# Five output banks, both rank-8 results in one bank, and the rank-8 result's low part made on GpSimd

## The reference

```python
# layer 3 (the last): rank-8 update of a base matrix, per batch
xw = gelu(layernorm(cond) @ w1 + b1) @ w2 + b2
x_a, x_b = split(xw)                          # (16, 512, 8) each
layer = base_layer + x_a[b] @ x_b[b].T        # per batch b
out = x3 + x3 @ layer
```

## Time and profile before

| | |
|---|---|
| median of 3 runs | 1496.57 us (1495.63 to 1499.19) |
| profiled execution | 1498.06 us, of which span 1496.1 us |
| busy in the span | TensorE 1422.0 us (95%), VectorE 1006.8, GpSimd 682.1, ScalarE 659.6 |
| mean granted TensorE clock | 0.977 of full speed |

### The profile page before, as it was taken

How to read it: one execution, slowest core, us unless ns; L and a number is a source line. 1 busy time by engine, 2 the same in 40 slices (tenths; PEclk the granted TensorE clock), 3 DMA queues, 4 the chain that set the end, 5 groups by cost and what they waited for, 6 DMA issues and landing times.

```text
span 1496.1 us, 49921 instructions
## 1 busy us (share of the span) xinstructions
PE 1422.0 (95%) x21159; PEld 1124.8 (75%) x21159; DVE 1006.8 (67%) x2707; ACT 659.6 (44%) x2185; POOL 682.1 (46%) x536
## 2 busy tenths in 40 slices
PE   6789999999999999999999999999997996999998
PEld 4457888888888888888888888888886874677776
DVE  4333757575757576767676666666656689898884
ACT  3444444545454545444444444444444442233332
POOL 2422444444444444434353535343424355777773
PEclk9799999999999999999999999999997997999999
DMA  9660142423232323333333323242315457888893
GB/s 351 225 245 18 33 84 41 76 49 68 52 65 52 66 51 66 58 59 58 59 61 62 64 54 67 53 70 52 58 31 107 113 112 139 284 316 308 315 329 124
DMA packets 441904, 168.15 MB, mean 112 GB/s; under 512 B 406433, under 2 KB 409633, under 8 KB 438354
## 3 DMA queue, kind: packets, MB, share of 16 engines
q1 hardware_dynamic: 441682, 164.97, 43.6%
HBM read 96.78 MB, written 68.16 MB: 110 GB/s over the span
## 4 chain that ended last, share of the span: by engine, by line
PE 90%; DVE 3%; issue 2%; ACT 2%; POOL 1%; DMA 1%; SPq 0%; ACTq 0%; DVEq 0%; POOLq 0%
PE bank L466 47%; PE recb L432 28%; PE bank L627 12%; PE bank L641 1%; PE bank L513 1%; DMA xt<-in_Wx 1%; ACT gates L813 1%; PE recb L610 1%; PE spare L610 1%; PE aux L478 1%; DVE pre L1150 0%; DVE pre L1148 0%; DVE hs L1155 0%; DVE pout L1214 0%; ACT hs L652 0%
## 5 line engine op out<-in xcount | busy, mean ns | idle before, releaser
L432 PEld LDWEIGHTS recb<-hs,scanS 128*128 128x128 f16 x16384 | 444.7, 96 | 172.6 <-DVE hs L1155 169.8
L432 PE MATMUL recb<-hs,scanS 128*128 128x32 f16 x16384 | 495.3, 177 | 25.9 <-DVE hs L1155 25.9
L652 ACT ACTIVATE hs<-pre 128x64 f16<-128x64 f32 x512 | 131.6, 257 | 621.6 <-DVE pre L1150 620.1
L1148 DVE TENSOR_TENSOR pre<-recb,xw 128x64 f32<-128x64 f32 x512 | 114.9, 224 | 266.6 <-PE recb L432 262.8
L1016 DVE RECIPROCAL gates<-gates 128x64 f32<-128x64 f32 (+1 forms) x484 | 258.1, 554 | 0.4
L1155 DVE TENSOR_TENSOR hs<-konst,hs 128x64 f16<-128x64 f32 x512 | 115.0, 225 | 137.0 <-ACT konst L653 137.0
L875 POOL TENSOR_TENSOR xt<-xt,hbuf 128x512 f32<-128x512 f32 (+1 forms) x65 | 98.8, 1520 | 177.7 <-ACT hbuf L656 177.7
L863 POOL TENSOR_TENSOR x1lo<-xt,x1hi 128x512 fp32r<-128x512 f32 x62 | 80.6, 1301 | 198.8 <-ACT x1hi L662 198.8
L881 POOL TENSOR_TENSOR gates<-gates 128x512 f32<-128x512 f32 x64 | 83.0, 1296 | 165.4 <-DVE gates L1016 165.4
L890 POOL TENSOR_TENSOR xt<-xt,pout 128x512 f32<-128x512 f32 x64 | 76.2, 1191 | 149.6 <-DVE pout L1042 144.5
L1150 DVE TENSOR_TENSOR pre<-recb,pre 128x64 f32<-128x64 f32 x512 | 114.8, 224 | 17.6
(11 more groups left out here) (202 smaller groups left out, 2730.4 us busy)
## 6 DMA issues: line engine op xcount, KB each, us to landing
xt<-in_x SPq DMA_DIRECT2D x64, 256.0 KB, 3.5
g_d<-gst SPq DMA_DIRECT2D x64, 256.0 KB, 3.8
n_d<-nst SPq DMA_DIRECT2D x64, 256.0 KB, 3.1
x_d<-xt SPq DMA_DIRECT2D x64, 256.0 KB, 3.1
out<-gates SPq DMA_DIRECT2D x64, 256.0 KB, 6.5
xt<-x_d SPq DMA_DIRECT2D x28, 512.0 KB, 4.6
stage<-in_w SPq DMA_DIRECT2D x11, 1024.0 KB, 5.8
xt<-g_d SPq DMA_DIRECT2D x14, 512.0 KB, 6.9
```

The costliest lines, as they stand in the source:

```text
L432: last = nc.tensor.matmul(rec[:, m].rearrange("p a b -> p (a b)"), w[:, k, m * P:(m + 1) * P], hs[:, k].rearrange("p a b -> p (a b)"), sta ...
L652: nc.scalar.activation(hs[:, :, 0, :], pre[t % 2][:], ACT.Tanh, scale=unscale).then_inc(s_h, 1)
L1148: nc.vector.tensor_tensor(pre0[:], rec[:, :, 0, :], xw[j % 2][:, t], ALU.add).then_inc(s_pre0, 1)
```

## The change

It makes five banks for the output of the last stage (`obank`: the four and `spare`); quarter t of batch b lies in bank (4b + t) mod 5. Both rank-8 results lie in `recb`, at columns 0 to 127 and 256 to 383. ScalarE makes, beside the high part, a second, whole copy of the rank-8 result in SBUF (`yf`), since GpSimd reads it there, and GpSimd makes the low part from it. The subtraction leaves VectorE's order and stands in GpSimd's behind `x3_low` of the next batch's chunk 1 (for batch 0 behind that of chunk 0).

```diff
--- before.py
+++ after.py
@@ -151,8 +151,13 @@
         scan = [scanS[k // 2][:, k % 2, :] for k in range(4)]
         oout = gates[:, 0:NT]
         ysh, ysl = ([x2hi[:, q, e * P:(e + 1) * P] for q in range(2)] for e in range(2))
+        yf = [xar[:, q * P:(q + 1) * P] for q in range(2)]
         xbs = [x2lo[:, q, :] for q in range(2)]
-        yp = [s[:, 0:P] for s in (recb, spare)]
+        yp = [recb[:, 0:P], turned]
+        obank = bank + [spare]
+
+        def quarter(b, t):
+            return obank[(NT * b + t) % len(obank)]
 
 
         (d_cond, d_w1, d_w2, d_wx, d_wh, d_rows, d_ln, d_h1, d_bias, d_c2, d_f, d_i, d_c) = (
@@ -174,8 +179,8 @@
         d_e = {k: [sem(f"t_d_e{k}{q}") for q in range(2)] for k in "gnx"}
         d_t = {k: [[sem(f"t_d_{k}{q}{h}") for h in range(2)] for q in range(2)] for k in "gnx"}
         d_xbs, d_out = [sem(f"t_d_xbs{q}") for q in range(2)], [sem(f"t_d_out{t}") for t in range(NT)]
-        (s_gc, s_nc, s_xc, s_one2, s_S, s_u, s_H, s_x3, s_x3h, s_x3l, s_pm, s_yp, s_yh, s_yl, s_op, s_o) = (
-            sem("t_" + s) for s in "s_gc s_nc s_xc s_one2 s_S s_u s_H s_x3 s_x3h s_x3l s_pm s_yp s_yh s_yl s_op s_o".split())
+        (s_gc, s_nc, s_xc, s_one2, s_S, s_u, s_H, s_x3, s_x3h, s_x3l, s_pm, s_yp, s_yh, s_yf, s_yl, s_op, s_o) = (
+            sem("t_" + s) for s in "s_gc s_nc s_xc s_one2 s_S s_u s_H s_x3 s_x3h s_x3l s_pm s_yp s_yh s_yf s_yl s_op s_o".split())
 
         made = {"x": s_xp, "f": s_f, "i": s_i, "c": s_c}
 
@@ -598,10 +603,8 @@
                 q = b % 2
                 pe.wait_ge(s_x3, C * b + m + 1)
                 if m == 0:
-                    if b >= 2:
-                        pe.wait_ge(s_yl, b - 1)
-                    elif b:
-                        pe.wait_ge(s_P, 2 * C * NBLK)
+                    if b:
+                        pe.wait_ge(s_yf, b)
                     else:
                         pe.wait_ge(s_x3, C)
                         pe.wait_ge(s_xah, 1)
@@ -617,14 +620,16 @@
                 pe.wait_ge(s_x3h, C * b + m + 1)
                 pe.wait_ge(s_x3l, C * b + m + 1)
                 for t in range(NT):
-                    if m == 0 and b:
-                        pe.wait_ge(s_o, NT * (b - 1) + t + 1)
+                    if m == 0 and NT * b + t == len(bank):
+                        pe.wait_ge(s_P, 2 * C * NBLK)
+                    elif m == 0 and b:
+                        pe.wait_ge(s_o, NT * b + t - len(bank))
                     elif m == 0:
                         kind, chunk = LAST_GROUPS[2 * C + t]
                         pe.wait_ge(emptied(kind), C * (NBLK - 1) + chunk + 1)
                     tok = slice(t * P, (t + 1) * P)
                     for e, (x3, w) in enumerate(((x3hi, bhi), (x3lo, bhi), (x3hi, blo))):
-                        last = nc.tensor.matmul(bank[t][:], x3[q][:, m, tok], w[:, m, :], start=(m == 0 and e == 0), stop=False)
+                        last = nc.tensor.matmul(quarter(b, t)[:], x3[q][:, m, tok], w[:, m, :], start=(m == 0 and e == 0), stop=False)
                 last.then_inc(s_pm, 1)
 
             for b in range(B):
@@ -638,7 +643,7 @@
                 for y, rows in ((ysh, PAIR), (ysl, RANK)):
                     for t in range(NT):
                         part = slice(t * PADB, t * PADB + rows)
-                        last = nc.tensor.matmul(bank[t][:], y[b % 2][part], xbs[b % 2][part], start=False, stop=(y is ysl), tile_position=(t * PADB, 0))
+                        last = nc.tensor.matmul(quarter(b, t)[:], y[b % 2][part], xbs[b % 2][part], start=False, stop=(y is ysl), tile_position=(t * PADB, 0))
                         if y is ysl:
                             last.then_inc(s_op, 1)
 
@@ -805,12 +810,15 @@
                 else:
                     act.wait_ge(s_c, C * NBLK)
                 nc.scalar.copy(ysh[b % 2], yp[b % 2]).then_inc(s_yh, 1)
+                if b >= 2:
+                    act.wait_ge(s_yl, b - 1)
+                nc.scalar.copy(yf[b % 2], yp[b % 2]).then_inc(s_yf, 1)
 
             def put_out(b, t):
                 act.wait_ge(s_op, NT * b + t + 1)
                 if b:
                     act.wait_ge(d_out[t], 16 * b)
-                nc.scalar.copy(oout[:, t, :], bank[t][:]).then_inc(s_o, 1)
+                nc.scalar.copy(oout[:, t, :], quarter(b, t)[:]).then_inc(s_o, 1)
 
             last = NBLK - 1
             for m in range(C):
@@ -959,6 +967,11 @@
                 pool.wait_ge(s_x3h, k + 1)
                 nc.gpsimd.tensor_tensor(x3lo[b % 2][:, m, :], xin[b % 2][:, m, :], x3hi[b % 2][:, m, :].bitcast(F32), ALU.subtract).then_inc(s_x3l, 1)
 
+            def y_low(b):
+                pool.wait_ge(s_yh, b + 1)
+                pool.wait_ge(s_yf, b + 1)
+                nc.gpsimd.tensor_tensor(ysl[b % 2], yf[b % 2], ysh[b % 2].bitcast(F32), ALU.subtract).then_inc(s_yl, 1)
+
             last = NBLK - 1
             for m in range(C // 2):
                 x2_low(last, m)
@@ -985,14 +998,20 @@
             for k in range(C, C + 3):
                 times_n(k)
             x3_low(C)
+            y_low(0)
             times_n(C + 3)
             x3_low(C + 1)
             times_n(C + 4)
             for k in range(C + 5, SLOTS):
                 times_n(k)
                 x3_low(k - 3)
+                if (k - 3) % C == 1:
+                    y_low((k - 3) // C - 1)
             for k in range(SLOTS - 3, SLOTS):
                 x3_low(k)
+                if k % C == 1:
+                    y_low(k // C - 1)
+            y_low(B - 1)
 
         @block.vector
         def _(dve):
@@ -1194,10 +1213,6 @@
                 dve.wait_ge(s_H, k + 1)
                 nc.vector.tensor_tensor(xin[b % 2][:, m, :], xin[b % 2][:, m, :], total, ALU.add).then_inc(s_x3, 1)
 
-            def y_low(b):
-                dve.wait_ge(s_yh, b + 1)
-                nc.vector.tensor_tensor(ysl[b % 2], yp[b % 2], ysh[b % 2].bitcast(F32), ALU.subtract).then_inc(s_yl, 1)
-
             def shares_of(m):
                 gate_sum(last, m)
                 recip(last, m, 0, PIECES)
@@ -1252,7 +1267,6 @@
             hidden(3)
             suffix(C)
             suffix(C + 1)
-            y_low(0)
             hidden(C)
             suffix(C + 2)
             hidden(C + 1)
@@ -1264,9 +1278,6 @@
                 if k + 3 < SLOTS:
                     suffix(k + 3)
                 hidden(k)
-                if k % C == 1:
-                    y_low(k // C - 1)
-            y_low(B - 1)
 
 
 def flat(view):
```

## The result

The changed kernel took 1488.17 us (median of 16 runs, 1485.7 to 1495.02) against 1500.63 for the kernel before in the same comparison: ratio 0.9922, 95% interval 0.9906 to 0.9938, so 0.8% faster. The profiled execution took 1486.39 us with a span of 1484.6 (before: 1498.06 and 1496.1).

What follows compares the result with a forecast made beforehand. Bound: TensorE plus a 0.72 us turnaround at each last-stage batch's end. Gains of 0.6 us at the start and 13 x 0.70 made 9.7 us, so 1486.9 us from the 1496.57 median; range 1483.8 to 1492, chance 0.62.

Steps and rivals of the forecast that it cites:

- Part 1: Handover between last-stage batches: with five output banks quarter 0 needn't wait for a drain, gaining 0.70 us each.
- Part 2: Rank-8 low part moves from VectorE to GpSimd: 0.60 us subtraction there, one more ScalarE copy, no cost to the period.
- the room: Slack between GpSimd's new subtraction and TensorE's rank-8 matmuls in each last-stage batch: 0.22 us.
- The sum: Whole last stage: 0.6 us at its start plus 13 transitions of 0.70 us, 9.7 us gained.
- The start: Batches 0 to 2 of the last stage: batch 2 starts 0.6 us sooner, bounds 0 to 1.5.
- (a): GpSimd's line becomes the last stage's bound: gain of 4.5 to 8 us, chance 0.18; smaller gains share 0.13 with (c).
- (b): Denser transfers in the last stage make n loads land 2 us later, delaying GpSimd: 1506.1 us, chance 0.07.
- (c): Last-stage handover: a later drain holds quarter 1 instead of quarter 0, 1493 to 1497 us; chance 0.13 shared with (a)'s end.
- (d): Denser TensorE work in the last stage lowers the clock; left out, given no size or chance.

Runs made afterwards that it cites:

- one drain more: The changed kernel with one more ScalarE copy of quarter 0 ahead of each batch's first drain, to a place nobody reads: ratio 0.9988 to the kernel before.
- both runs: The changed kernel with one or three more GpSimd subtractions of the same size ahead of each low part: ratios 0.9955 and 1.0008 to the kernel before.
- the banks alone: The changed kernel with VectorE keeping the low part, so only five banks and the shared rank-8 bank: ratio 0.9953 to the kernel before.

## Why the prediction was right

**Time and sign.** Forecast 1486.9 from a median of 1496.57, 0.65% less; the ratio says 0.78% (0.62 to 0.94). 0.65 lies in the interval. The stage alone gained 10.6 us, forecast 9.7. That 1486.9 is so near the measured 1488.17 is in part luck: the kernel before was 4.1 us slower in this comparison than the median that the forecast started from (1500.63 against 1496.57), and the gain was 12.5 in place of 9.7.

**Part 1, 0.70 us a handover.** Measured: from the start of batch 2 to the rank-8 matmuls of batch 15, 191.61 before and 181.94 after, 9.67 / 13 = 0.74. Quarter 0 starts where it was put (0.67 after the start of the rank-8 matmuls). Quarter 1 was put 0.83 behind it with the weights loaded late, its second matmul another 0.31 later; they came after 0.80 and 0.27. So the term was small by 0.04: the release after the drain was taken as 0.14 from the chain, but quarter 1 starts 0.11 after the drain's end (0.06 with one drain more), and TensorE doesn't stand for it.

**Part 2.** GpSimd's subtraction takes 0.46 to 0.47, not 0.60; the room was put at 0.22, and with the 0.14 shorter subtraction that is 0.36, which is what both runs gave. ScalarE's second copy costs nothing that shows, as said. What the prediction missed is here: it put VectorE's 1.32 us of waiting down as "neither is on the path". With four banks that is right, with five it is wrong by 0.27 us a batch. The wait was not slack: the turn with ScalarE was 1.14 us of a loop of 13.32, the next bound below 13.79. The sum held only because the change removed both, and the prediction had put the second at nothing: in that it was lucky. Its step "VectorE's 12.06 us now lie free below 13.09" was true of the busy time and would have misled about the banks alone, as my expectation for them did.

**The start, 0.6 us.** Measured 0.9 (37.78 before, 36.87 after from the stage's first product to batch 2). The waits came where they were put: the rank-8 matmuls of batch 0 at 19.74 us of the stage, forecast 1280.65 - 1260.79 = 19.86; those of batch 1 at 36.20, forecast 36.48. As in the forecast, the gain is the handover from batch 1 to batch 2 (1.50 before, 0.67 after): batch 1's rank-8 matmuls stood at 36.28 before, so all that happens ahead of them gained 0.1. That VectorE is no longer held there brought nothing. It is a balance of two things. Before, TensorE's 13 products behind the wait of 2.90 us ran at a granted clock of 0.50, 0.43 us apart in place of 0.23, some 2.6 us lost (13 x 0.20, an estimate), and it then ended batch 1 without a wait:

```profile
1282.00:1287.70 5.70, 5.67 (x13) 4.45 (x14) 5.57 (x7) 0.62 (x1) 4.66 (x4) 0.50 0.99 374
```

After the change only some six products are slow, but TensorE waits for GpSimd, 0.89 us at batch 1's end. The prediction gave the clock nothing because GpSimd ends that batch. After the change that is right; the time before it was compared with had the clock in it.

**The rivals.** (a) GpSimd's line: the room was real and is 0.36 us; it did not bind in the steady batches. (b) The transfers: the share rose to 0.93, the n loads land as before (medians over 1310 to 1414 us: 8.2 and 8.4, before 8.5 and 8.3), and GpSimd waits for none. The room of 0.3 us that the prediction gave them was too small and its price too high: with 512 KB more they land 1.4 and 1.7 us later and TensorE is late in three batches, with 1 MB more 2.9 and 2.8 later, and that costs 0.3 us a batch, where the prediction had a period 0.78 us above that of the kernel before for a landing 2 us later. Why so little comes through is not shown. Some of VectorE's work does wait for g loads now, since it runs ahead of need. (c) and (d): no drain was late, the clock stayed at 1.00 with TensorE busy for all of 104 us.

## What to carry to other kernels

When a wait at the end of a stage's period is removed, look for the next loop, not for the next busiest engine: work out for each engine its operations plus every turn in which it waits for an answer to its own last result. Such a turn looks like harmless idle time as long as a longer loop hides it. It can be broken by moving the work to another engine or, as here with no work added anywhere, by letting the answering engine do the old request before the new one.

## What the runs showed of the hardware

A DMA busy share near 1 in these profiles was not yet the limit of the rate: 0.93 at 333 GB/s, 1.01 at 369 and 1.03 at 402, over the same stretch of the same stage, with one load of 512 KB or 1 MB more a batch as the only difference between the kernels. It was not free either: the n loads landed 1.4 and 2.9 us later (into `late`), and the stage took 1.5 and 3.8 us more. GpSimd subtracts 128x128 in 0.46 us out of plain rows in SBUF, against 0.605 for the strided addition of that size and 1.29 for four times the width; from the first and the last an estimated 0.46 - (1.29 - 0.46) / 3 = 0.18 us of it do not depend on the width. ScalarE drains a bank while TensorE writes into others in the time that it takes with TensorE standing: 0.59 us for the first of four, 0.58 before the change, and 2.05 for the four, 2.06 before. TensorE's granted clock was 0.50 for 5.7 us behind a wait of 2.90, and its 128x512 products then stood 0.43 us apart in place of 0.23.
